# A new order of operations in the nine sparse steps of a cross-attention and mixture-of-experts kernel

## The chip, the cores and the metric

The kernel runs on one core of a Trainium2 chip. A core has five engines with queues of their own: TensorE (matmuls and transposes, written to PSUM), VectorE, ScalarE, GpSimd, and SyncE, which issues DMAs; GpSimd and ScalarE issue some too. They are ordered only by semaphores: an instruction raises a counter when it is done, and another queue waits for a count. The metric is the device time of one execution in microseconds, as the median over several.

## The reference, cut to what matters

```python
x = x + _L0_xattn_ref(_layernorm(x), ctx, ...)   # one head over 1601 context rows
x = x + _L0_ffn_ref(_layernorm(x), ...)          # "B", below
x = x + _L1_xattn_ref(_layernorm(x), ctx, ctx, mask, ...)
x = x + _L1_ffn_ref(_layernorm(x), ...)

def _L0_ffn_ref(x, w_q, w_k, w_gate, value_experts, output_experts):   # HEADS, DIM_HEAD, EXPERTS = 8, 64, 8
    q, k = x @ w_q, x @ w_k                      # 8 heads of 64
    gates = sigmoid(x @ w_gate)                  # an expert for each token and head
    gm = one_hot(argmax(gates)) * gates
    values = einsum('bhne,ehdk,bnd->bhnk', gm, value_experts, x)
    attn = softmax(causal(q * SCALE @ k.T))
    out = einsum('bhij,bhjk->bhik', attn, values)
    return einsum('bhne,ehkd,bhnk->bhnd', gm, output_experts, out).sum(axis=1)
```

x is 4 x 512 x 256. Each token and head picks one of 8 value experts and one of 8 output experts, the same for both.

## The kernel before

The program goes through five stages one after another; the change lies in `attentions_ab` (L439), which does the first attention (A) and B for the four batches in turn. The order of each engine's queue is written out by hand.

**Batches and steps.** Batch b does `attention_a`, then `attention_b`. B takes the 8 heads as four pairs; a step p handles pair p, and Q = 4b + p numbers the steps. In batches 0 to 2, steps 0 to 2 are `sorted_pair` (the nine sparse steps) and step 3 is `last_pair`, which runs beside the start of the next batch's attention A. Batch 3 applies the output experts densely (`pair`, `ending_pair`).

**What a sparse step does on TensorE** (`sorted_pair`, L1214): it turns step p's exponentials (`turn_b`, six parts through PSUM banks 3 and 4), multiplies them with the values (`values`, bank 5), turns the result back (`turn_rows`, bank 4), makes the scores of step p+1 (`scores_b`, three parts, banks 0 and 1), and makes the next step's values for all eight experts in eight units (`unit`, four matmuls of 512 columns). In sparse steps every unit writes bank 2 and waits until VectorE has read the unit before it (`pe.wait_ge(val_mul, U)`, L1112). Between these it turns the sorted rows of step Q-1 (`turn_sorted`, three parts, banks 3 and 4) and multiplies them with the experts' blocks (`out_sorted`, six chunks, banks 6 and 7).

**VectorE** reads units (a product with the gates, L1579, then a sum over experts, L1583), copies parts 1, 3 and 5 of the turned attention (`turned_b`, L1759), reduces the scores' maxima (`maxima`, L1570), makes the rows' weights (`weigh`, L1664, L1668), writes the weighted rows (`write_rows`, L1678, which raises `rows_v`), adds gathered rows to x (`add_back`, L1688, two additions for each of four token tiles), and in step 0 works out where each row goes (`place`, pieces 1 at L1647 to L1653 and 2 at L1658). **ScalarE** copies parts 0, 2 and 4 (L1421), the turned sorted rows (`read_sorted`, L1426) and `boT`, the attention's result (L1474), takes exponentials (`probabilities`, L1413), and copies and stores the chunks (`read_blocks`, L1443, L1446).

**The way of the sorted rows.** When `rows_v` says that step Q's rows are written, GpSimd scatters them to DRAM in the order of their experts (`scatter`, eight indirect DMAs, L716); SyncE loads them as `inS` (`load_sorted`, L628, shown as oxB<-sorted_in); in step Q+1 TensorE turns and multiplies them; ScalarE stores the chunks; in step Q+2 and after GpSimd gathers each token's rows (`gather`, L733), and VectorE adds them. In GpSimd's queue a step is gather (two tiles of Q-2), scatter of Q, gather (the other two). Each gather waits until an earlier one's buffer has been added. In SyncE's queue `load_experts` (L617) issues 22 copies of expert blocks ahead of each `load_sorted`.

The waits that matter, in `values` and in `unit`:

```python
pe.wait_ge(pT_a, 3 * (Q + 1))            # ScalarE's copies, parts 0, 2, 4
pe.wait_ge(pT_v, 3 * (Q + 1))            # VectorE's copies, parts 1, 3, 5
if p == 0 and b < SORTED:
    pe.wait_ge(placed, PLACING * b + 6)  # place piece 1, its first result
...
if u >= 2 * NT:
    pe.wait_ge(val_mul, U)               # VectorE's product of the unit before
```

Of the kernel before, what the change touches and what calls it, by code (L numbers as in the profile page):

```python
# [38 lines left out]
PAIRS = HB // 2  # L39
SORTED = NB - 1  # L40
# [398 lines left out]
def attentions_ab(k, A):  # L439
# [37 lines left out]
    EARLIER = PAIRS * SORTED  # L477
    with ExitStack() as own:
# [321 lines left out]
        def _(pe):  # L800
# [198 lines left out]
            def turn_rows(b, p):  # L999


                Q = PAIRS * b + p
                pe.wait_ge(bo_ev, Q + 1)
                pe.wait_ge(pT_v, 3 * (Q + 1))
                if Q:
                    pe.wait_ge(sorted_a, 3 * (Q - 1) + 2)
                for t in range(NT):
                    mm = pe.transpose(ps[:, 4, t * P:(t + 1) * P], boT[:, t * P:(t + 1) * P], k.ident[:, :])
                mm.then_inc(rows_mm, 1)

            def turn_sorted(Q, g):
# [6 lines left out]
                else:  # L1018
                    pe.wait_ge(exped, NT * (Q // PAIRS + 2))
                    pe.wait_ge(pt_v, 2 * NT * (Q // PAIRS + 2))  # L1020
                if g == 2:
                    pe.wait_ge(sorted_a, 3 * Q + 1)
# [191 lines left out]
            def sorted_pair(b, p):  # L1214
# [9 lines left out]
                if Q:  # L1224
                    turn_sorted(Q - 1, 0)
                scores_b(b, p + 1, 0)
                unit(b, u + 2)
                values(b, p)
                if Q:
                    turn_sorted(Q - 1, 1)  # L1230
                unit(b, u + 3)
                turn_rows(b, p)
                if Q:
# [118 lines left out]
        def _(act):  # L1352
# [96 lines left out]
            def attention_b(b):  # L1449
# [11 lines left out]
                for p in range(PAIRS):  # L1461
# [3 lines left out]
                    if behind:  # L1465
                        read_sorted(Q - 1, 0)
                    if more:
                        probabilities(b, p + 1, 0)
# [3 lines left out]
                    elif Q:  # L1472
                        act.wait_ge(gated, EB * (Q - EARLIER))
                    nc.scalar.copy(boT[:, :], ps[:, 5, :]).then_inc(bo_ev, 1)  # L1474
                    if behind:
                        read_sorted(Q - 1, 1)
# [25 lines left out]
        def _(v):  # L1502
# [328 lines left out]
            def sorted_pair(b, p):  # L1831
# [5 lines left out]
                turned_b(b, p, 5)  # L1837
                weigh(b, p)
                maxima(b, p + 1, 0)
                if p == 0:  # L1840
                    place(b, 1)
                unit(b, u + 2)
                if p and Q >= 3:
                    add_back(Q - 3, 2)
                    add_back(Q - 3, 3)
                if p == 0:
                    place(b, 2)
                unit(b, u + 3)
                write_rows(b, p)
                unit(b, u + 4)  # L1850
# [1368 lines left out]
```

## Time and profile before

| | us |
|---|---|
| median of 3 runs | 2068.59 (2065.03 to 2076.61) |
| profiled execution, its own time | 2065.59 |
| its span in the profile | 2063.6 |
| TensorE busy | 1900.1 (92%) |
| VectorE busy | 1241.6 (60%) |
| ScalarE busy | 980.4 (48%) |
| GpSimd busy | 751.0 (36%) |
| mean granted TensorE clock | 0.973 |
| first sparse step starts, last one ends | 221.8, 771.8 |

A row of the timeline is the start, the length, the engine (PE is TensorE, DVE VectorE, ACT ScalarE, POOL GpSimd, SPq SyncE's queue), the line, the operation with output and input, its shape and count; brackets hold the idle time before it and what ended it. Consecutive instructions of one line are merged. A TensorE row's length includes the way through the array, so the next row can start before it ends; the distance of starts is what an operation takes of the queue. The program's names are those of buffers that several tiles share: oxB holds experts' blocks, rows, `inS`; og_or_pT holds the turned sorted rows and places; val_or_prob the values and the gathered rows; vx_or_keys the value experts. The granted clock is given as a share of full speed.

### The profile page before, as it was taken

Reading aid. Unit: us, or ns where it says so; the run is one execution under the profiler, and the core shown is the slowest. Engines: PE = TensorE matmul, PEld = TensorE weight load, DVE = VectorE, ACT = ScalarE, POOL = GpSimd, SP = SyncE. Lnnn points to the kernel's source line nnn. Section 1 sums busy time; section 2 is a strip of 40 time slices with the busy share of each in tenths; the row PEclk is TensorE's granted clock in tenths of the full one; section 3 lists DMA queues with packets and bytes.
Section 4 is the critical chain, followed back from the end, with each engine's and each line's share of the span. In section 5 each row is a group of like instructions: output and inputs, shape, how many; then the busy total and the mean of one; then the engine's idle time right before and its main releaser. Section 6 shows DMA issues by size and latency. Waiting matters only on the chain. (4 is left out here: it accounts for less than half of the span.)

```text
span 2063.6 us, 29289 instructions
## 1 busy us (share of the span) xinstructions
PE 1900.1 (92%) x10024; PEld 1008.8 (49%) x10024; DVE 1241.6 (60%) x2514; ACT 980.4 (48%) x1899; POOL 751.0 (36%) x702
## 2 busy tenths in 40 slices
PE   8989898999899998899989999999999999986993
PEld 5666445744475446646643333433433343335772
DVE  5423753366535663388777777778777777742332
ACT  3412243224422343221138888778877977951220
POOL 4221335225532453111044233326433621426674
PEclk9999999999999999999999999999999999987997
DMA  8841147217621464422236383345345532114987
GB/s 286 221 169 64 49 153 243 70 29 221 199 99 48 141 207 159 159 48 78 32 98 124 103 245 78 83 96 153 84 82 138 119 58 40 57 58 160 300 177 166
DMA packets 166028, 262.87 MB, mean 127 GB/s; under 512 B 46983, under 2 KB 105173, under 8 KB 164600
## 3 DMA queue, kind: packets, MB, share of 16 engines
q1 hardware_dynamic: 121208, 179.21, 32.1%
q0 software_dynamic: 26624, 47.18, 9.1%
q10 hardware_dynamic: 18048, 34.61, 4.6%
q8 instruction: 80, 1.31, 0.3%
q14 instruction: 68, 0.56, 0.1%
HBM read 165.92 MB, written 104.44 MB: 131 GB/s over the span
## 5 line engine op out<-in xcount | busy, mean ns | idle before, releaser
L2672 ACT ACTIVATE d_prob<-ps 128x512 f32<-128x512 f32 (+1 forms) x832 | 473.6, 597 | 153.1 <-PE ps L2522 152.4
L2699 DVE CUSTOM_DVE_ANT_0 ps<-ps,maskN 128x801 f32<-128x801 f32 x480 | 467.5, 1015 | 122.9 <-PE ps L2492 122.7
L1114 PE MATMUL ps<-vx_or_keys,b_xT 128*128 128x512 f32 x512 | 244.5, 605 | 7.8 <-DVE val_or_prob L1579 7.4
L2534 PE MATMUL ps<-d_prob,vaug 128*32 128x512 f32 (+1 forms) x1664 | 225.9, 609 | 0.3 <-ACT d_prob L2672 0.3
L2521 PE MATMUL ps<-maskT,identb 128*128 128x512 bf16 (+1 forms) x498 | 191.7, 385 | 3.8 <-POOL maskT L2396 1.9
L266 POOL DMA_INDIRECT table<-xr,slot x128 | 128.1, 1000 | 168.4 <-PE ps L2522 130.7
L2668 ACT CAST ps<-maskT 128x512 f32<-128x512 bf16 (+1 forms) x310 | 185.5, 598 | 0.0
L733 POOL DMA_INDIRECT val_or_prob<-sorted_out,oxB x96 | 98.7, 1028 | 186.7 <-DVE xx L1688 114.0
L1579 DVE TENSOR_TENSOR val_or_prob<-ps,b_gm 128x512 f32<-128x512 f32 x128 | 88.3, 690 | 97.5 <-PE ps L1114 97.4
L1413 ACT ACTIVATE prob_or_gate<-ps,b_mx 128x512 f32<-128x512 f32 (+3 forms) x128 | 66.1, 525 | 152.5 <-DVE b_mx L1570 145.4
L716 POOL DMA_INDIRECT sorted_in<-oxB x96 | 95.6, 996 | 116.7 <-issue 57.1
L1114 PEld LDWEIGHTS ps<-vx_or_keys,b_xT 128*128 128x128 f32 x512 | 89.7, 190 | 97.8 <-issue 75.5
L1583 DVE TENSOR_REDUCE val_or_prob<-val_or_prob 128x64 f32<-128x512 f32 x128 | 132.5, 1035 | 4.4
L2396 POOL TENSOR_SCALAR maskT<-c_rawT 128x512 bf16<-128x512 int32 (+1 forms) x52 | 100.1, 1925 | 49.5 <-PE ps L2522 44.2
L2522 PE MATMUL ps<-raw,kS 99*128 99x512 bf16 (+1 forms) x312 | 116.1, 388 | 1.4 <-ACT ps L2668 1.4
L2521 PEld LDWEIGHTS ps<-maskT,identb 128*128 128x128 bf16 (+1 forms) x498 | 49.6, 100 | 120.4 <-issue 33.6
L1443 ACT COPY og_or_pT<-ps 128x1024 f32<-128x1024 f32 x66 | 62.2, 942 | 84.1 <-PE ps L1048 79.6
L2522 PE MATMUL ps<-qS,vx_or_keys 99*128 99x512 bf16 (+1 forms) x260 | 98.6, 383 | 1.9 <-ACT ps L2668 1.9
L2522 PE MATMUL ps<-vx_or_keys 99*128 99x512 bf16 (+1 forms) x260 | 98.3, 382 | 1.9 <-ACT ps L2668 1.9
L816 PE MATMUL ps<-maskN,kS 128*128 128x512 f32 (+1 forms) x256 | 96.5, 523 | 1.7 <-PEq L104 1.7
L848 PE MATMUL ps<-og_or_pT,raw 128*128 128x128 f32 (+1 forms) x832 | 97.6, 275 | 0.0
L848 PEld LDWEIGHTS ps<-og_or_pT,raw 128*128 128x128 f32 (+1 forms) x832 | 95.4, 192 | 1.5 <-issue 1.5
(357 smaller groups left out, 3156.1 us busy)
## 6 DMA issues: line engine op xcount, KB each, us to landing
sorted_out<-og_or_pT ACTq DMA_DIRECT2D x55, 512.0 KB, 3.1
oxB<-in_B_ox SPq DMA_DIRECT2D x264, 64.0 KB
c_rawT<-in_maskT SPq DMA_DIRECT2D x24, 512.0 KB
vx_or_keys<-k_parts SPq DMA_DIRECT2D x60, 200.1 KB, 7.2
k_parts<-x_k SPq DMA_DIRECT2D x16, 600.4 KB
table<-xr POOLq DMA_DIRECT2D x16, 578.0 KB
e_buf<-table SPq DMA_DIRECT2D x32, 289.0 KB, 3.7
oxB<-sorted_in SPq DMA_DIRECT2D x12, 704.0 KB, 6.3
```

What stands on the lines that cost most here:

```text
L266: g.indirect_dma_start(out=k.table[:, :], out_offset=bass.IndirectOffsetOnAxis(ap=k.slot[:, j:j + 1], axis=0), in_=k.xr[:, t, :], in_offse ...
L733: g.indirect_dma_start(out=back[:, t % 2, a, :], out_offset=None, in_=k.sorted_out[Q % 2][:, :], in_offset=bass.IndirectOffsetOnAxis(ap=to ...
L848: mm = pe.matmul(ps[:, 6, m * P:(m + 1) * P], k.ctxNA[0:KW[i], i, m * P:(m + 1) * P], pT[0:KW[i], i, :], start=i == 0 and m == 0, stop=i = ...
L1114: mm = pe.matmul(ps[:, bank, :], xTB[:, c, t * P:(t + 1) * P], vxB[:, c, h, :], start=c == 0, stop=c == NC - 1)
L1583: v.tensor_reduce(val[:, t, h // 2 % 2, h % 2, :], tmp[:, u % 2, :].rearrange("p (e d) -> p d e", e=EB), AX_X, ALU.add).then_inc(val_sum, 1)
L2396: g.tensor_scalar(maskT[0:KW[i], i, :], rawT[0:KW[i], u % 2, i % 2, :], 0.0, MASKED, ALU.is_equal, ALU.mult).then_inc(biasT, 1)
L2521: pe.matmul(ps[0:w, BANKS[u], :], k.identb[0:w, 0:w], maskT[0:w, i, :], start=True, stop=False)
L2522: pe.matmul(ps[0:w, BANKS[u], :], kS[G % NS][0:KROWS + 3, h, i * P:i * P + w], qS[G % NS][0:KROWS + 3, h, :], start=False, stop=True, skip ...
L2534: mm = pe.matmul(ps[VW * h:VW * (h + 1), ACC, :], vaug[0:w, G % 2, i, h, :], prob[0:w, T % 2, h, :], start=i == 0, stop=i == NKT - 1)
L2668: nc.scalar.copy(ps[0:w, BANKS[later], :], maskT[0:w, i, :]).then_inc(mask_a, 1)
L2672: nc.scalar.activation(prob[0:w, T % 2, h, :], ps[0:w, BANKS[GH * T + h], :], ACT.Exp, scale=SCALE_C).then_inc(exped, 1)
L2699: v.tensor_tensor_reduce(banks, banks, maskN[:, t, MO[half]:MO[half] + w], 1.0, -3.0e38, ALU.add, ALU.max, mp[:, t, h, half:half + 1]).the ...
```

## The change

It changes the order inside `sorted_pair` on TensorE and VectorE, and of two operations in ScalarE's loop.

- TensorE: `values` goes ahead of the scores' first part, `turn_rows` follows the scores, and then come unit u+2, `turn_sorted` 1, unit u+3, `turn_sorted` 2 and unit u+4. `turn_rows` writes the bank that `turn_sorted` 1 uses, so it now waits only for the sorted rows of the step before last (except in `last_pair`), and `turn_sorted` 1 waits for `write_rows`.
- ScalarE: in batches 0 to 2 the copy to `boT` goes ahead of the exponentials of the scores' first part.
- VectorE: `place` 1 goes ahead of `weigh`; the left additions of step Q-3 (tiles 2 and 3) go ahead of the maxima; `write_rows` goes behind the maxima and ahead of unit u+2.

```diff
@@ -1003,7 +1003,7 @@
                 pe.wait_ge(bo_ev, Q + 1)
                 pe.wait_ge(pT_v, 3 * (Q + 1))
                 if Q:
-                    pe.wait_ge(sorted_a, 3 * (Q - 1) + 2)
+                    pe.wait_ge(sorted_a, 3 * (Q - 1) + (2 if p == PAIRS - 1 else 0))
                 for t in range(NT):
                     mm = pe.transpose(ps[:, 4, t * P:(t + 1) * P], boT[:, t * P:(t + 1) * P], k.ident[:, :])
                 mm.then_inc(rows_mm, 1)
@@ -1018,6 +1018,8 @@
                 else:
                     pe.wait_ge(exped, NT * (Q // PAIRS + 2))
                     pe.wait_ge(pt_v, 2 * NT * (Q // PAIRS + 2))
+                if g == 1 and (Q + 1) % PAIRS < PAIRS - 1 and Q + 1 < EARLIER:
+                    pe.wait_ge(rows_v, Q + 2)
                 if g == 2:
                     pe.wait_ge(sorted_a, 3 * Q + 1)
                 for i, j in enumerate(range(4 * g, min(4 * g + 4, BLOCKS))):
@@ -1223,13 +1225,13 @@
                 turn_b(b, p, 5)
                 if Q:
                     turn_sorted(Q - 1, 0)
+                values(b, p)
                 scores_b(b, p + 1, 0)
+                turn_rows(b, p)
                 unit(b, u + 2)
-                values(b, p)
                 if Q:
                     turn_sorted(Q - 1, 1)
                 unit(b, u + 3)
-                turn_rows(b, p)
                 if Q:
                     turn_sorted(Q - 1, 2)
                 unit(b, u + 4)
@@ -1464,7 +1466,7 @@
                     read_turned(Q)
                     if behind:
                         read_sorted(Q - 1, 0)
-                    if more:
+                    if more and b == SORTED:
                         probabilities(b, p + 1, 0)
                     act.wait_ge(bpv_mm, Q + 1)
                     if 1 <= Q <= EARLIER:
@@ -1472,6 +1474,8 @@
                     elif Q:
                         act.wait_ge(gated, EB * (Q - EARLIER))
                     nc.scalar.copy(boT[:, :], ps[:, 5, :]).then_inc(bo_ev, 1)
+                    if more and b < SORTED:
+                        probabilities(b, p + 1, 0)
                     if behind:
                         read_sorted(Q - 1, 1)
                         read_sorted(Q - 1, 2)
@@ -1835,18 +1839,18 @@
                 turned_b(b, p, 3)
                 unit(b, u + 1)
                 turned_b(b, p, 5)
-                weigh(b, p)
-                maxima(b, p + 1, 0)
                 if p == 0:
                     place(b, 1)
-                unit(b, u + 2)
+                weigh(b, p)
                 if p and Q >= 3:
                     add_back(Q - 3, 2)
                     add_back(Q - 3, 3)
+                maxima(b, p + 1, 0)
+                write_rows(b, p)
+                unit(b, u + 2)
                 if p == 0:
                     place(b, 2)
                 unit(b, u + 3)
-                write_rows(b, p)
                 unit(b, u + 4)
                 maxima(b, p + 1, 1)
                 unit(b, u + 5)
```

## Rows read from the trace of the kernel before

**Rows 1.** The page's first part: busy time of each engine.

```profile
PE 1900.1 (92%) x10024; PEld 1008.8 (49%) x10024; DVE 1241.6 (60%) x2514; ACT 980.4 (48%) x1899; POOL 751.0 (36%) x702
```

**Rows 2.** TensorE's waits, 225 to 900 us: total, times, longest.

```profile
PE ps L1024 <- DMA oxB<-sorted_in: 9.4, 5, 2.5
```

**Rows 3.** TensorE's timeline in batch 1, step 1: start, length, instructions, idle before.

```profile
475.83 1.98 PE L1114 MATMUL ps<-vx_or_keys,b_xT 128*128 128x512 f32 x4 [0.15 <-DVE val_or_prob L1579]
...
483.48 0.63 PE L1024 MATMUL ps<-ident,oxB 128*128 128x128 f32 x4 [0.33 <-ACT b_pT L1421]
484.04 1.13 PE L957 MATMUL ps<-b_kT,b_qT 64*128 64x512 f32 x4
...
485.22 1.94 PE L1114 MATMUL ps<-vx_or_keys,b_xT 128*128 128x512 f32 x4
487.09 2.37 PE L1083 MATMUL ps<-b_pT,val_or_prob 128*64 128x512 f32 x16
489.39 0.66 PE L1024 MATMUL ps<-ident,oxB 128*128 128x128 f32 x4
489.89 1.88 PE L1114 MATMUL ps<-vx_or_keys,b_xT 128*128 128x512 f32 x4
491.61 0.60 PE L1008 MATMUL ps<-ident,b_oT 128*128 128x128 f32 x4
492.04 0.49 PE L1024 MATMUL ps<-ident,oxB 128*128 128x128 f32 x3
492.55 1.98 PE L1114 MATMUL ps<-vx_or_keys,b_xT 128*128 128x512 f32 x4
```

**Rows 4.** VectorE's timeline in the same step.

```profile
484.20 0.55 DVE L1759 COPY b_pT<-ps 128x384 f32<-128x384 f32 x1
...
485.42 1.23 DVE L1570 TENSOR_REDUCE b_mx<-ps 128x2 f32<-128x1024 f32 x1 [0.36 <-PE ps L962]
487.20 0.69 DVE L1579 TENSOR_TENSOR val_or_prob<-ps,b_gm 128x512 f32<-128x512 f32 x1 [0.55 <-PE ps L1114]
...
488.89 1.86 DVE L1688 TENSOR_TENSOR xx<-xx,val_or_prob 128x256 f32<-128x256 f32 x4
...
493.49 0.68 DVE L1678 TENSOR_TENSOR oxB<-ps,b_gr 128x512 f32<-128x512 f32 x1
```

**Rows 5.** ScalarE's timeline in the same step.

```profile
489.51 0.59 ACT L1474 COPY b_oT<-ps 128x512 f32<-128x512 f32 x1 [1.32 <-PE ps L1083]
```

**Rows 6.** TensorE's timeline at two of the five waits for sorted rows.

```profile
258.99 0.66 PE L1024 MATMUL ps<-ident,oxB 128*128 128x128 f32 x4 [2.48 <-DMA oxB<-sorted_in]
...
548.41 1.11 PE L1024 MATMUL ps<-ident,oxB 128*128 128x128 f32 x4 [1.63 <-DMA oxB<-sorted_in]
549.32 2.90 PE L816 MATMUL ps<-maskN,kS 128*128 128x512 f32 x4
```

**Rows 7.** TensorE's, then VectorE's timeline in batch 0, step 0.

```profile
228.31 0.82 PE L983 MATMUL ps<-ident,prob_or_gate 128*128 128x128 f32 x6
...
237.71 1.99 PE L1114 MATMUL ps<-vx_or_keys,b_xT 128*128 128x512 f32 x4 [0.35 <-DVE val_or_prob L1579]
...
230.17 0.55 DVE L1759 COPY b_pT<-ps 128x384 f32<-128x384 f32 x1
...
232.08 0.41 DVE L1647 SCALAR_TENSOR_TENSOR og_or_pT<-og_or_pT,ps 128x256 f32<-128x256 f32 x1
```

**Rows 8.** SyncE's queue, expert copies and the sorted load behind them.

```profile
255.12 28.57 SPq L617 DMA_DIRECT2D oxB<-in_B_ox  x22
286.45 0.37 SPq L628 DMA_DIRECT2D oxB<-sorted_in  x1
```

**Rows 9.** GpSimd's timeline, last gather behind batch 1, step 0's scatter.

```profile
479.60 1.01 POOL L733 DMA_INDIRECT val_or_prob<-sorted_out,oxB  x1 [0.30 <-issue]
```

**Rows 10.** Windows: PE, PEld, DVE, ACT, POOL busy (instructions), granted clock, DMA share, GB/s.

```profile
548.00:552.00 4.00, 3.59 (x8) 1.92 (x8) 0.82 (x2) 0.59 (x1) 0.00 (x0) 0.58 0.68 243
258.00:262.00 4.00, 3.01 (x13) 1.47 (x14) 1.41 (x4) 0.59 (x1) 0.00 (x0) 1.00 0.22 62
```

## The prediction

> **What bounds the kernel now.** The first part of the page says that TensorE is busy for 1900.1 of 2063.6 us [rows 1], so an edit counts only where it moves TensorE. The change touches only the nine sparse steps (batches 0 to 2, steps 0 to 2, 221.8 to 771.8 us) and, through its transfers, the last step of each batch. So I read the list of what TensorE waited for from 225 to 900 us, then its timeline through one step, then VectorE's and ScalarE's timelines beside it, then the queues of GpSimd and SyncE that bring the sorted rows back.
>
> The list shows five waits of 9.4 us in total for the sorted rows, before `turn_sorted` part 0 [rows 2]. They stand at 259.0 (2.48 us), 324.0 (2.49), 548.4 (1.63), 712.9 (0.38) and 777.8 (2.42); two are shown [rows 6]. They are all that earlier rows can give back. The other waits of a step (two transposed banks, the sorted chunks' copies) are not touched.
>
> Step 1 of batch 1 shows the pattern. TensorE goes from `turn_sorted` 0 (483.48) through scores, unit u+2, values, `turn_sorted` 1, unit u+3, the rows and `turn_sorted` 2 to unit u+4 at 492.55 without a wait [rows 3]: 9.07 us. The old order uses the scores and a unit to cover VectorE's last copy of transposed attention (484.20 to 484.75) [rows 4], and uses values and the rows to keep units u+2, u+3 and u+4 apart. All three share PSUM bank 2, so each waits for VectorE's product of the one before.
>
> **The change, part by part.** I walk the same step in the new order with the same rows.
>
> *Values ahead of the scores.* `turn_sorted` 0 lets the next operation start at 484.04. Values needs VectorE's copy of part 5, which ends at 484.20 + 0.55 = 484.75; TensorE follows such a release after 0.05 us (VectorE's product at 0.04 us after a unit's end is the same size). Values starts at 484.80: **0.76 us new**.
>
> *Rows ahead of the unit.* Values takes 2.30 us to the next start (487.09 to 489.39), scores 1.18 (484.04 to 485.22), the rows 0.43 (491.61 to 492.04) [rows 3]. Scores start at 487.10, the rows at 488.28, unit u+2 at 488.71. ScalarE's copy of the attention (0.59 us) [rows 5] starts when values ends, at about 487.2, and is over by 487.8, before the rows need it: it now stands ahead of the exponentials, so nothing is ahead of it. The exponentials move behind it and are wanted only by the scores' second part, some 8 us later. No cost.
>
> *Units closer together.* Unit u+2 ends 1.88 us after its start [rows 3, 4], at 490.59. The product runs 490.63 to 491.32 (0.69 us) and frees bank 2 at 491.37. TensorE, with only `turn_sorted` 1 between (unit 1.72 to the next start, transposes 0.50), is there at 490.93: **0.44 us new**. A unit after a wait lasts 1.98 us (475.83), so u+3 ends at 493.35, its product at 494.08, and u+4 starts at 494.13, while u+3 (1.72 to the next start) and `turn_sorted` 2 (0.51) would let it start at 493.60: **0.4 to 0.5 us new**. Before it started at 492.55. The step is 1.6 us longer, and from u+4 on nothing differs: units and chunks there are released by the same copies in the same order.
>
> *VectorE's moves.* The maxima start 1.38 us after the scores (484.04 to 485.42) and take 1.23 [rows 4], so they run 488.48 to 489.71 and `write_rows` (0.68) ends at 490.4. The new wait of `turn_sorted` 1 on these rows (TensorE at 490.43) is about met, the narrowest term: if write_rows is late by x, x comes on top, but u+3 hides the first 0.44. Behind it stand only those transposes and the units. The left additions (four, 1.86 us from 488.89) [rows 4] now follow the weights at about 485.1 and end by 487.0, inside the time until the maxima can start. Their last gather was issued by 480.6 [rows 9] and stands behind the step before's scatter, which also moves up, and no wait was seen on them. I take them at nothing; had the rows landed only at 488.9, the maxima would end some 2 us late in four steps, 6 us in all. Done earlier, they let GpSimd's next gather, and the scatter queued behind it, start some 4 us earlier.
>
> *Step 0 of a batch.* Values also waits for `place` 1's first result, which now comes right behind the copy. That operation takes 0.41 us [rows 7], 0.33 more than the copy alone, since neighbours on VectorE overlap by about 0.09: 1.9 us for step 0 of batches 1 and 2. In the very first step there is no `turn_sorted`. The transposes leave TensorE free at 228.31 + 0.74 = 229.05, the copy ends at 230.72, the result at 231.04: 2.04 us of idling. With no transposes between the units either, u+2 starts at 235.0, u+3 at 237.65 and u+4 at 240.4 in place of 237.71 [rows 7]: 2.7 us.
>
> Sum of the new waits: 2.7 + 2 x 1.9 + 6 x 1.6 = **16.1 us**.
>
> *What comes back.* `write_rows` moves from 493.49 to about 489.7 within its step, so scatter and load may move 3.8 us. But SyncE issues 22 expert copies (28.57 us, 255.12 to 283.69) ahead of the load, which went out at 286.45 once the scatter had landed [rows 8]; it can move at most 2.8 us there. TensorE itself arrives later: at 258.99 - 2.48 + 2.7 = 259.2 for the first wait [rows 6], past even the old landing; 3.4, 5.1, 1.9 and 4.7 us later at the others. So all five waits go: **-9.4 us**. One of them was followed by a stretch at a granted clock of 0.58, between the two levels of 1.2 and 2.4 GHz [rows 10]: the next batch's scores at 549.32 last 2.90 where four such matmuls last 1.88. With the transposes (1.11 for 0.66) that costs 1.4 us [rows 6]. The stretch around 259, after the 2.48 us wait, stays at 1.00. I count its loss as a gain, **-1.4 us**, between 0 and 1.4.
>
> Between batches, TensorE waits 2.37 us at 582.9 for GpSimd's normalised tile. That waits for the last stored chunk, which moves with TensorE, so it stays.
>
> Net: 16.1 - 9.4 - 1.4 = **+5.3 us**. The profiled execution took 2065.59 us (span 2063.6); the sum makes it 2070.9. The median of the runs is 3.0 us above the profiled one, so the predicted median is 2068.6 + 5.3 = **2073.9 us**, 0.26% more. The three runs lie 11.6 us apart; about 0.5% (10.3 us) is what a measurement of this kernel can tell from no change.
>
> **Rivals.** (a) *The short waits cost TensorE its clock, and it is slower.* The place is the stretch from `turn_sorted` 0 to u+4, where each step's waits grow by 1.6 us. One such stretch at 0.58 costs 1.4 us by [rows 6, 10]; with one in each of the nine steps it is 13 us more, 2087. It passes 0.5% from four such steps on. For it: the 1.63 us wait did so. Against it: the 2.48 us wait did not. Chance 0.13.
> The Trainium skill, "TensorE: Matmul & The Clock Gate", section "A second HAM failure mode: psum-queue depth-cycling", says that short idling between groups of matmuls that cycle through banks makes the clock swing and lowers throughput. By that rule this change, which makes a single bank the pace of three units, would be rival (a). By the rows of the steps, which wait at bank 2 already, it would be my sum.
>
> (b) *The bank does not pace the units.* Only the wait before values is real: 6 x 0.76 + 2 x 1.09 + 2.04 = 8.8 us, minus 10.8: 2066.6, no change. For it: the copies and products on which it rests are a few tenths apart, and missing records could hide slack. Against it: the same release is seen at 475.83 with 0.15 us, where one short chunk stands between units. Chance 0.17.
>
> (c) *The transfers come no earlier and TensorE still waits at them.* The load stands behind 22 expert copies; if these start later as the step grows, the five waits stay: 2068.6 + 16.1 = 2084.7. It decides when a load lands over 3 us later after its step's start than now. Against it: a step is longer by less than TensorE's arrival moves. Chance 0.06.
>
> (d) *No new wait at all*, the transposed attention being ready in time: 2068.6 - 10.8 = 2057.8. The copy's end at 484.75 speaks plainly against it. Chance 0.03.
>
> **Numbers.** The forecast has 0.61, with its own range of 2067 to 2081 (bounds: a clock stretch more or less at 1.4 us each, narrow waits a few tenths in nine steps, up to 6 us for the additions). To leave out no more than 2 in 10, the range runs over (b) and most of (a) and (c): 2062 to 2085. Faster by over 0.5% (under 2058.3): (d) and a tail of (b), 0.05. Slower (over 2078.9): most of (a), all of (c) and the tail of the forecast, 0.18. Same 0.77.
>
> **What would show it.** In the changed profile, values should wait 0.6 to 0.8 us for VectorE's transposed copy in eight steps and about 2 in the first; units u+3 and u+4 should each show 0.2 to 0.45 us behind VectorE's product; the wait for sorted rows before part 0 should be gone; steps should run some 34.5 us where 32.9 stands now; the load should go out right behind the 22nd expert copy. The prediction is wrong if turn_sorted 1 waits for `write_rows` by much more than 0.2 us (then maxima or additions are late), if load waits persist, or if the granted clock in the steps falls under 0.95.

## The result, and the profile after

The changed kernel took 2095.11 us (median of 4 runs, 2084.77 to 2104.28) and the kernel before, beside it, 2066.81 (2064.11 to 2076.61). The ratio is 1.0133, with a 95% interval of 1.0100 to 1.0166: 1.3% slower, outside the range of the prediction. The profiled execution took 2097.95 us. The four runs of the changed kernel spread with the clock: the fastest had a mean granted clock of 0.973, the slowest 0.965.

The page's first part for the changed kernel (busy time of each engine) answers to [rows 1]:

```profile
PE 1903.9 (91%) x9944; PEld 1017.9 (49%) x10024; DVE 1242.0 (59%) x2514; ACT 979.6 (47%) x1899; POOL 752.8 (36%) x702
```

TensorE does the same work in a span of 2096.0 us in place of 2063.6. The time lies in what it waited for, from 225 to 900 us, in the same view as [rows 2] (total, times, longest):

```profile
PE ps L983 <- ACT og_or_pT L1445: 16.5, 6, 5.0
PE ps L1116 <- DVE val_or_prob L1583: 13.0, 25, 1.2
...
PE ps L1085 <- issue: 4.5, 6, 0.8
PE ps L1085 <- DVE og_or_pT L1651: 4.3, 3, 2.1
```

The same view of the kernel before has these two lines for the first and the second:

```profile
PE ps L1114 <- DVE val_or_prob L1579: 5.5, 9, 1.2
...
PE ps L983 <- ACT og_or_pT L1443: 2.3, 3, 0.8
```

The wait for the sorted rows, 9.4 us before, has left the list. The waits of units and of values have grown as forecast. The first line was not in the forecast: the first transposes of a step (`turn_b` 0) wait 16.5 us for ScalarE's copy of the sixth chunk, where they waited 2.3. ScalarE in turn waits for the landing of its own stores, 20.4 us in 8 places; the second line is the kernel before:

```profile
ACT og_or_pT L1445 <- DMA sorted_out<-og_or_pT: 20.4, 8, 4.3
```

```profile
ACT og_or_pT L1443 <- DMA sorted_out<-og_or_pT: 1.5, 1, 1.5
```

**Inside a step it went as worked out.** TensorE's timeline in batch 1, step 1 of the changed kernel, which answers to [rows 3]:

```profile
493.78 0.63 PE L1026 MATMUL ps<-ident,oxB 128*128 128x128 f32 x4 [0.33 <-ACT b_pT L1423]
495.16 2.37 PE L1085 MATMUL ps<-b_pT,val_or_prob 128*64 128x512 f32 x16 [0.75 <-issue]
497.46 1.13 PE L957 MATMUL ps<-b_kT,b_qT 64*128 64x512 f32 x4
498.52 0.29 PE L962 MATMUL ps<-causal,identb 128*128 128x128 bf16 x2
498.64 0.61 PE L1008 MATMUL ps<-ident,b_oT 128*128 128x128 f32 x4
499.09 1.88 PE L1116 MATMUL ps<-vx_or_keys,b_xT 128*128 128x512 f32 x4
500.81 0.63 PE L1026 MATMUL ps<-ident,oxB 128*128 128x128 f32 x4
501.75 1.98 PE L1116 MATMUL ps<-vx_or_keys,b_xT 128*128 128x512 f32 x4 [0.31 <-DVE val_or_prob L1583]
503.57 0.49 PE L1026 MATMUL ps<-ident,oxB 128*128 128x128 f32 x3
504.52 1.98 PE L1116 MATMUL ps<-vx_or_keys,b_xT 128*128 128x512 f32 x4 [0.46 <-DVE val_or_prob L1583]
```

Values waits 0.75 us. The list calls this wait "issue", but VectorE's copy of part 5 ends 0.1 us before its end (494.51 + 0.55 = 495.06), as forecast:

```profile
494.51 0.55 DVE L1763 COPY b_pT<-ps 128x384 f32<-128x384 f32 x1
```

Unit u+3 waits 0.31, unit u+4 0.46, and `turn_sorted` 1 at 500.81 waits for nothing. The step's units start at 486.12 and the next step's at 520.73: 34.6 us, where the prediction had some 34.5.

**At the end of a step it did not.** First TensorE, then ScalarE at the end of batch 0, step 2 and the start of step 3 of the changed kernel:

```profile
325.66 0.70 PE L1050 MATMUL ps<-oxB,og_or_pT 64*128 64x256 f32 x4
329.68 1.06 PE L983 MATMUL ps<-ident,prob_or_gate 128*128 128x128 f32 x7 [3.32 <-ACT og_or_pT L1445]
330.99 3.44 PE L983 MATMUL ps<-ident,prob_or_gate 128*128 128x128 f32 x13 [0.25 <-ACT b_pT L1423]
334.22 1.06 PE L1026 MATMUL ps<-ident,oxB 128*128 128x128 f32 x4
335.07 2.96 PE L816 MATMUL ps<-maskN,kS 128*128 128x512 f32 x4
```

```profile
322.66 0.37 ACTq L1448 DMA_DIRECT2D sorted_out<-og_or_pT  x1
323.93 1.01 ACT L1445 COPY og_or_pT<-ps 128x1024 f32<-128x1024 f32 x1 [1.30 <-DMA sorted_out<-og_or_pT]
...
328.95 0.59 ACT L1445 COPY og_or_pT<-ps 128x512 f32<-128x512 f32 x1 [2.55 <-DMA sorted_out<-og_or_pT]
```

The sixth chunk has been multiplied at 326.36 (325.66 + 0.70). ScalarE copies it only at 328.95, because it copies into two buffers by turns, and this chunk's still holds the fourth chunk until its store, issued at 322.66, has landed: 6.2 us later (328.9). `turn_b` 0 waits for all copies of the step before (`pe.wait_ge(blocks_a, CHUNKS * (Q - 1))`), so TensorE waits too. The reason is in SyncE's queue, which answers to [rows 8]:

```profile
292.91 28.16 SPq L617 DMA_DIRECT2D oxB<-in_B_ox  x22
321.19 0.54 SPq L628 DMA_DIRECT2D oxB<-sorted_in  x1
```

The load of the sorted rows (704 KB) goes out right behind the 22nd expert copy, as forecast, and so ahead of the stores of the fourth, fifth and sixth chunk. The view of DMA issues (KB each, median us from issue to landing) shows it, for 12 us at this place of the changed kernel (318 to 330), then of the kernel before (309 to 321):

```profile
sorted_out<-og_or_pT ACTq DMA_DIRECT2D x3, 512.0 KB, 5.6
oxB<-sorted_in SPq DMA_DIRECT2D x1, 704.0 KB, 6.1
```

```profile
sorted_out<-og_or_pT ACTq DMA_DIRECT2D x3, 512.0 KB, 2.9
oxB<-sorted_in SPq DMA_DIRECT2D x1, 704.0 KB, 6.7
```

The three 512 KB stores of the changed kernel are those of the third, fourth and fifth chunk. The third's was issued at 319.98, 1.2 us ahead of the load, and landed after 3.9 us; the two behind the load took 6.2 and 5.6. In the kernel before, the load went out at 317.24, 0.6 us before the next step's first transposes, and behind all three of these stores, the last of which was issued at 315.63.

**The granted clock** (level 2.4 GHz at 1.00; 1.2 GHz would be 0.50) fell behind some of these waits. Windows of the changed kernel, with the columns of [rows 10]:

```profile
234.70:239.00 4.30, 4.25 (x18) 2.13 (x20) 1.07 (x4) 0.14 (x1) 0.00 (x0) 0.60 0.17 49
329.50:338.00 8.50, 7.93 (x30) 5.23 (x30) 3.69 (x9) 2.17 (x5) 1.02 (x1) 0.60 0.30 93
493.00:506.00 13.00, 11.15 (x54) 5.50 (x51) 9.20 (x15) 4.05 (x9) 7.09 (x7) 1.00 0.34 102
```

The first lies behind the 2.06 us wait of the first step, the second behind the 3.32 us wait, and the third, with waits of 0.33, 0.75, 0.31 and 0.46, keeps its clock. I laid windows of 8 us over the whole stretch from the first sparse step's first transposes to batch 3's and added length times (1 - clock): 11.8 us before, 22.1 after. Of the latter 10.2 us stand behind the three long waits at `turn_b` (3.32 us at 329.68, 5.04 at 560.94 and 4.57 at 800.04); at these transposes the kernel before loses none. The other differences, each of 1.7 us or 3.4, cancel: new are the first step and two places near 600 and 822, gone are the load wait's at 548 and one near 407.

The 32.4 us by which the span grew are 24.9 in this stretch (677.8 to 702.7), 3.6 ahead of it and 3.9 behind it, where both kernels run the same instructions. The 3.6 are clock: from 185 to 200 us it is 0.77 in this profile and 1.00 in that of the kernel before. So a part of a profile's clock loss comes and goes between executions, whatever the order of the steps.

The length of a wait does not settle by itself whether the clock falls behind it. All versions with values ahead of the scores have the same 2.06 us wait in the first step. First the changed kernel, then run 1 below:

```profile
234.75 4.07 PE L1085 MATMUL ps<-b_pT,val_or_prob 128*64 128x512 f32 x16 [2.06 <-DVE og_or_pT L1651]
```

```profile
231.42 2.37 PE L1087 MATMUL ps<-b_pT,val_or_prob 128*64 128x512 f32 x16 [2.06 <-DVE og_or_pT L1653]
```

Values takes 2.37 or 2.38 us in the profiles of runs 1, 2, 3 and 6, and 4.07 and 4.06 in the changed kernel's and run 5's, which are also the two of these six with 0.77 at 185 to 200 us. Why that is so stays open.

### The profile page after: what moved, and what is told of

Same layout as the page of the kernel before. It is cut to its first block and busy times, and to the rows that moved or that the text cites. A ratio compares the mean times of both kernels' runs of the same rounds, so it can differ in the third digit from the quotient of the medians.

```text
span 2096.0 us, 29217 instructions
## 1 busy us (share of the span) xinstructions
PE 1903.9 (91%) x9944; PEld 1017.9 (49%) x10024; DVE 1242.0 (59%) x2514; ACT 979.6 (47%) x1899; POOL 752.8 (36%) x702
## 5 line engine op out<-in xcount | busy, mean ns | idle before, releaser
L1116 PE MATMUL ps<-vx_or_keys,b_xT 128*128 128x512 f32 x512 | 244.8, 606 | 15.0 <-DVE val_or_prob L1583 14.4
L2525 PE MATMUL ps<-maskT,identb 128*128 128x512 bf16 (+1 forms) x425 | 163.6, 385 | 1.8 <-DVE d_oN L2735 1.7
```

Of the source, the lines that this page charges most:

```text
L1116: mm = pe.matmul(ps[:, bank, :], xTB[:, c, t * P:(t + 1) * P], vxB[:, c, h, :], start=c == 0, stop=c == NC - 1)
L2525: pe.matmul(ps[0:w, BANKS[u], :], k.identb[0:w, 0:w], maskT[0:w, i, :], start=True, stop=False)
```

## The experiments

Three theories went in. **Theory 1**: the early load shares the transfers' bandwidth with the last chunk stores, and a full store buffer passes the delay on to TensorE. **Theory 2**: the left additions, moved ahead, move the gathers, and these hold ScalarE's copies up. **Theory 3**, rival (a) of the prediction: the short waits in the steps cost the clock. Diffs are against the changed kernel where nothing else is said.

**1. The load held behind the last chunk** (SyncE, ahead of the load):

```diff
+                    if p < PAIRS - 1:
+                        sp.wait_ge(blocks_mm, CHUNKS * Q)
                 sp.dma_start(inS, ...)
```

> The changed kernel, with one more wait in SyncE's queue: in steps 0 to 2 the load of the sorted rows goes out only when TensorE has finished the last chunk of the step before. Theory 1 (the load, 704 KB and now issued some 3 us ahead of the last two chunk stores, makes these stores land late; ScalarE's copy of the last chunk waits for a buffer, and the next step's first transposes wait for that copy): the 16.5 us of waits before the first transposes fall to about 2.3 us as in the kernel before, the waits for the sorted rows come back in the three last steps (about 2.3 us each), and the time falls by 10 to 15 us, to about 2080 us. Theory 2 (GpSimd's gathers and scatters, which moved up too, slow the stores): the waits stay near 16 us and the time near 2095 us. Theory 3 (the clock alone costs it): neither the waits nor the time change.

Measured: 2085.49 us against 2070.2, ratio 1.0056 (1.0034 to 1.0078). TensorE's waits in its profile:

```profile
PE ps L1028 <- DMA oxB<-sorted_in: 8.4, 6, 2.8
...
PE ps L985 <- ACT og_or_pT L1447: 2.4, 3, 0.9
```

The 16.5 us are back at 2.4, and the load waits at 8.4. ScalarE's waits for its stores are back at 2.9 us in 3 places. The gathers and additions keep their places (at the end of batch 0, step 2 the first gather is issued 0.57 us behind the fourth chunk's first matmul in both kernels, at 316.21 and 321.00), and the 512 KB stores there take 3.6 us in place of 5.6. So it is the early load that makes `turn_b` wait, and not the gathers.

**2. The additions back behind unit u+2.**

```diff
-                if p and Q >= 3: add_back(Q - 3, 2); add_back(Q - 3, 3)   # ahead of the maxima
+                if p and Q >= 3: add_back(Q - 3, 2); add_back(Q - 3, 3)   # behind unit(b, u + 2)
```

> The changed kernel with the left additions of step Q-3 back behind unit u+2. Gathers and scatters of steps 5, 6, 9 and 10 start some 5 us later and so does the load behind them; step 2 of batch 0 has no such additions. Theory 1 (load against stores): the 3.3 us wait at the end of batch 0 stays, those of batches 1 and 2 (1.4, 5.0, 1.75, 4.6 us) shrink to near zero, in all 8 to 12 us less, about 2085 us. Theory 2 (gathers against stores): the gathers of tiles 2 and 3 of the step before last move back too, so all shrink but batch 0's, which cannot be told from theory 1 here; the two differ in the first experiment. Theory 3: no change from 2095 us.

Measured: 2086.9 us, ratio 1.0079 (1.0048 to 1.0110). The wait at `turn_b` is 5.8 us in 4 places, a load wait of 6.1 us is there again, and ScalarE's copies wait 11.4 us in 4 places for gathers, which they hardly do in the changed kernel:

```profile
PE ps L1026 <- DMA oxB<-sorted_in: 6.1, 2, 3.2
PE ps L983 <- ACT og_or_pT L1445: 5.8, 4, 2.6
...
ACT og_or_pT L1445 <- DMA val_or_prob<-sorted_out,oxB: 11.4, 4, 3.7
```

With the additions late, GpSimd reaches the scatter late, the load goes out later and collides less: in the last steps of batches 1 and 2 the wait at `turn_b` is 0.78 us and the load waits are 3.15 and 2.97; in batch 0, which has no such additions, `turn_b` still waits 2.57 us, where I had expected 3.3. Both theories forecast that the waits shrink, so this run alone does not tell them apart. With run 1 it says that the moved additions let the load go early enough to cause the wait.

**3. The rows back behind unit u+3, values still ahead.**

```diff
                 scores_b(b, p + 1, 0)
-                turn_rows(b, p)
                 unit(b, u + 2)
                 if Q: turn_sorted(Q - 1, 1)
                 unit(b, u + 3)
+                turn_rows(b, p)          # write_rows on VectorE likewise
```

> The changed kernel with the turned rows and write_rows back behind unit u+3 (values still ahead of the scores, the copy of the attention and the additions still early). The rows are written about as late as before, so scatter and load are late again. Theory 1: no chunk waits beyond 2.3 us; in each step 0.74 us before values, 0.3 us before unit u+3, none before u+4; with waits for the sorted rows of some 2 us in the last steps: about 2067 + 9 to 12 = 2076 to 2079 us. Theory 2: the gathers ahead of the scatter are still early, so part of the chunk waits stay: 2085 us or more.

Measured: 2082.19 us, ratio 1.0051 (1.0036 to 1.0066). The wait at `turn_b` is 2.3 us in 3 places, the load waits 9.7 in 5, values' waits 7.3, units' 8.3. Without the earlier rows, nothing of the new wait is left, and neither is anything of the gain. The time is some 3 us above what I had expected.

**4. The kernel before, with the additions alone moved ahead of the maxima** (the second diff the other way round, in the kernel before).

> The kernel before with only the left additions ahead of the maxima. GpSimd's gathers of steps 5, 6, 9 and 10 start some 4 us earlier, the scatter only 1 us (write_rows ends at 494.2 there). Theory 1: the load goes out 1 us earlier at most, the chunk waits stay near 2.3 us and the time within 4 us of 2067 us. Theory 2: early gathers alone bring chunk waits of several us, 2072 us or more.

Measured: 2070.85 us, ratio 0.9999 (0.9982 to 1.0016); load waits 10.2 us in 4 places, `turn_b` 2.3 in 3. Alone, this edit costs nothing and brings nothing.

**5. A buffer of its own for the sixth chunk** (512 floats a partition that nothing uses in these steps; not shown is a wait on VectorE that keeps the next batch's attention A from overwriting it before its store has landed):

```diff
+                own_buffer = c == 5 and (Q + 1) % PAIRS < PAIRS - 1 and not between
-                if n >= 2:
+                if n >= 2 and not own_buffer:
                     act.wait_ge(kept[c % 2], 16 * (n // 2))
-                o = outS[not between][c % 2]
+                o = last_out if own_buffer else outS[not between][c % 2]
```

> The changed kernel, with the sixth chunk of each sparse step copied to a buffer of its own, so that ScalarE's copy of it no longer waits for the store of the fourth chunk. The load goes out as early as in the changed kernel and meets the stores as before. Theory 1 (the early load delays the stores, and a store buffer that is not free delays the sixth copy and with it the next step's first transposes): TensorE's wait at turn_b for ScalarE's chunk copy falls from 16.5 us in 6 places to under 6 us, while the landing of the stores stays near 5.6 us where the load runs; the stretches of low clock behind the waits go as well, and the time falls by 8 to 14 us against the changed kernel, to 2081 to 2087. Rival (ScalarE reaches the sixth chunk late for another reason, as the exponentials behind the attention's copy or the gathers): the waits at turn_b stay above 12 us and the time stays at 2093 to 2097.

Measured: 2075.18 us (10 runs) against 2069.0, ratio 1.0029 (1.0007 to 1.0051). The chunk copy's line in TensorE's list, and the place of the 3.32 us wait:

```profile
PE ps L984 <- ACT og_or_pT L1447: 2.3, 3, 0.8
...
327.28 0.96 PE L984 MATMUL ps<-ident,prob_or_gate 128*128 128x128 f32 x7 [0.78 <-ACT og_or_pT L1447]
328.58 2.32 PE L984 MATMUL ps<-ident,prob_or_gate 128*128 128x128 f32 x13 [0.35 <-ACT b_pT L1424]
```

The load still goes out early (321.56) and the stores still take long (median 6.8 us from issue to landing between 318 and 334), but TensorE no longer waits for them, and ScalarE's waits for them fall from 20.4 us to 2.7. The 13 transposes take 2.32 us in place of 3.44, and of the clock loss in the stretch (22.1 us) 13.6 are left, none of them behind the first transposes. This is the decisive run: 16.5 us went to 2.3 by a buffer, and the ratio from 1.0133 to 1.0029, further than the 2081 to 2087 us that I had expected. The prediction's own sum, +0.26%, lies within its interval, which reaches from 0.07% to 0.51%. Its profile is of the slowest of the ten executions (2082.41 us).

**6. The x_mid store held until the last chunk is multiplied.** In step 2 of batches 1 and 2, SyncE issues a 512 KB store behind the load.

```diff
                         if p == 2 and b >= 1:
+                            sp.wait_ge(blocks_mm, CHUNKS * (PAIRS * b + p))
                             keep_x(b - 1)
```

> The changed kernel, with the 512 KB store of x_mid (step 2 of batches 1 and 2) held until TensorE has done the step's last chunk; the load of the sorted rows stays early. Theory 1 says that both transfers are in the way: the waits of 5.0 and 4.6 us at the start of the last steps of batches 1 and 2 fall to about 3.3, that of batch 0, which has no x_mid store; in all 16.5 goes to about 13.5, and the time to 2090 to 2094. Rival, the load alone is the cause: the waits stay at 5.0 and 4.6 and the time at 2095. Rival, the x_mid store is most of it: they fall under 1.5 us.

Measured: 2084.81 us, ratio 1.0096 (1.0071 to 1.0120); `turn_b` waits 11.9 us in 6 places, longest 3.3:

```profile
PE ps L984 <- ACT og_or_pT L1446: 11.9, 6, 3.3
```

The two longest waits (5.0 and 4.6) are gone to the level of batch 0, where there is no such store. So about 5 of the 16.5 us are the second transfer's. Against the kernel before, the time is 19.9 us longer in place of 27.5, so it fell by 7.6 us where I had expected 1 to 5, though the two intervals overlap. Behind those two waits the clock had fallen too (loss in the stretch 22.1 us after, 15.3 here).

**7 and 8. Another order, with and without the third buffer**, against the kernel before. Scores stay ahead of values; the rows go to bank 5, which values has left:

```diff
                 scores_b(b, p + 1, 0)
-                unit(b, u + 2)
                 values(b, p)
+                unit(b, u + 2)
+                turn_rows(b, p)          # bank 5; the next values waits for rows_v Q
                 if Q: turn_sorted(Q - 1, 1)
                 unit(b, u + 3)
-                turn_rows(b, p)
```

On VectorE `write_rows` follows unit u+2; the additions, `place` 1 and ScalarE's copy of the attention stay as early as in the changed kernel.

> A version of the kernel before that aims at the load waits alone. Scores stay ahead of values; unit u+2 follows values and the rows follow it, written to bank 5, which values has left, so that turn_sorted 1 need not wait for them; write_rows stands behind unit u+2 on VectorE, the left additions and place 1 ahead of the maxima, the copy of the attention ahead of the exponentials, and the sixth chunk has a buffer of its own. By the in-step walk: no wait before values, 0.43 us before u+4 in nine steps (3.9 us), write_rows about 2.3 us earlier than before, so the load leaves 2 us earlier and the five load waits (9.4 us) fall to under 2; with the stretch of low clock gone, 5 to 7 us faster than before, 2060 to 2065. If an early load costs even with the third buffer, or units are paced another way, it is the same as before or slower, 2066 to 2075.

> The same without the buffer of its own for the sixth chunk. Theory 1: the load is only 2 us earlier than in the kernel before and meets just the last one or two stores, so the waits at turn_b for the chunk copy are 2 to 6 us, more than in the kernel before (2.3) and less than in the changed one (16.5); the time is 0 to 4 us above the version with the buffer. Rival, the number of buffers does not matter: both versions take the same time and show the same waits at turn_b.

Measured: with the buffer 2072.0 us, ratio 1.0011 (0.9989 to 1.0032); without it 2069.99, ratio 1.0013 (0.9996 to 1.0029). The 4 us in front of u+4 are there in both (units' waits 9.2 and 9.8 us). A gain in time is not. With the buffer the load waits are 8.1 us in 4 places, without it 3.2 in 5. The wait at `turn_b` is 2.3 and 2.4 us, so here the number of buffers makes no difference, as the rival said, and the 2.4 us without it lie at the low end of what I had expected. SyncE's queue and TensorE at the last of them, with the buffer:

```profile
775.85 0.36 SPq L629 DMA_DIRECT2D oxB<-sorted_in  x1
776.27 2.22 SPq L604 DMA_DIRECT2D x_mid<-kS  x1
```

```profile
786.55 0.66 PE L1025 MATMUL ps<-ident,oxB 128*128 128x128 f32 x4 [3.58 <-DMA oxB<-sorted_in]
```

Issue to use is 10.7 us, where the kernel before had 6.4 at this place (771.40 to 777.79). Against the start of the step it was issued 3.1 us earlier (3.5 us ahead of it in place of 0.4) and used 1.2 us later (7.2 us behind it in place of 6.0). I had expected it to bring the waits under 2 us, and that was wrong: in this profile, beside stores and the x_mid store, the earlier issue was no earlier landing. It need not be so. Without the buffer the load went out as early at this place (770.23, 3.3 us ahead of the step), landed after 5.8 us, and nothing waited; there the stores took 8.8 us. That the two versions differ in this rests on one profile each, and I don't lay it to the buffer.

**9 to 12. On another chip.** The last runs fell on a chip where the kernel before itself takes 2190.14 us (2207.57 beside the last one), so they are read against runs of that chip alone.

Run 9 adds the suspected cause to the kernel before and moves nothing:

```diff
+                if Q and p < PAIRS - 1:
+                    sp.wait_ge(blocks_mm, CHUNKS * (Q - 1) + 4)
+                    sp.dma_start(k.x_mid[NB - 1], <512 KB of constants>).then_inc(extra, 16)
                 for half in scattered[Q % 2]: ...      # then the load
```

> The kernel before with one suspected cause added and nothing moved: in eight sparse steps SyncE issues a store of 512 KB (constant data to a DRAM buffer that is overwritten later) right behind the expert copies, when the fourth chunk has been multiplied, so some 3 us ahead of the load of the sorted rows. Theory 1 (a large transfer beside the last chunk stores delays them, and the full store buffer holds up the sixth copy and the next step's first transposes): the stores land about 1.3 us later (512 KB at some 390 GB/s), TensorE's wait at turn_b for the chunk copy rises from 2.3 us in 3 places to 5 to 12 us in 5 to 8 places, and the time by 3 to 12 us. Rival, that wait needs the changed order of copies and exponentials on ScalarE: it stays at 2.3 us and the time within 2 us, but for load waits that may grow by up to 1 us each.

Runs 10 to 12 hold the x_mid store until the load has landed, in the kernel before (10) and in the version of run 8 (11, and 12 once more):

```diff
                         if p == 2 and b >= 1:
+                            sp.wait_ge(ld_sorted, 16 * (PAIRS * b + p + 1))
                             keep_x(b - 1)
```

> The kernel before, with the x_mid store of batches 1 and 2 held until the load of the sorted rows has landed (they are issued 0.4 us apart). If transfers issued together share the bandwidth, the load lands about 1 us earlier in these two steps: the load waits at 548.4 (1.63 us) and 777.8 (2.42) fall to 0.5 to 1.4, and the low-clock stretch behind the first may go; 1 to 4 us faster, not to be told from no change. Rival: the load's landing does not depend on the store, and nothing moves.

> The version with the rows in bank 5 and two buffers, with the x_mid store held until the load has landed. Load waits fall from 3.2 us in 5 places to 1.5 to 2.5, and the waits at turn_b stay at 2.4; 2065 to 2070, the same as the kernel before within what can be told.

> The version with the rows in bank 5, two buffers and the x_mid store behind the load once more, in five rounds, on whatever chip is free. If it gains only where transfers are slow (the chip of the run before took 2190 us for the kernel before), then on a chip where the kernel before takes 2065 to 2070 us it is the same within 0.3%: load waits 9.4 to some 2 us, 4 us new before u+4, and 0 to 3 us more or less at the batch's end. If the gain of 1.0% is the version's own, it is 2045 to 2055.

Measured: run 9 2205.19 us, ratio 1.0051 (1.0018 to 1.0083); run 10 2182.03, 0.9961 (0.9921 to 1.0002); run 11 2162.05, 0.9896 (0.9811 to 0.9981); run 12 2169.8 against 2207.57, 0.9814 (0.9770 to 0.9858). The `turn_b` wait in run 9, and in run 10 (from 225 to 960 us), which is nearest to the kernel before on this chip:

```profile
PE ps L990 <- ACT og_or_pT L1450: 16.5, 8, 4.8
```

```profile
PE ps L1049 <- ACT og_or_pT L1444: 42.8, 19, 9.6
PE ps L1049 <- issue: 33.5, 11, 7.8
...
PE ps L984 <- ACT og_or_pT L1444: 6.0, 5, 1.6
```

An extra transfer ahead of the last stores raises the wait from 6.0 us in 5 places to 16.5 in 8, with no order changed, and the kernel is slower by 11 us (0.51% of 2190). ScalarE's copies wait 23.5 us for their own stores in place of 16.5, and 8.8 for gathers in place of 1.9. That has the sign and the size of Theory 1, but it weighs less than runs 1, 5 and 6: run 10 is only a stand-in for a profile of the kernel before on this chip, and this chip has waits of its own. `out_sorted` waits 76.3 us in run 10 (42.8 + 33.5), and ScalarE's list for the whole span of run 10 names something as the end of its idle time that the kernel before never shows on the first chip in its list:

```profile
ACT og_or_pT L1444 <- remote: 114.2, 19, 11.7
```

Such waits end late though the input is there ("remote" is the list's name for a releaser that the trace does not hold). In run 10 TensorE has done its scores at 584.78 (584.38 + 0.40), and VectorE starts their maxima at 593.46:

```profile
584.38 0.40 PE L963 MATMUL ps<-causal,identb 128*128 128x128 bf16 x4
```

```profile
593.46 1.29 DVE L1571 TENSOR_REDUCE b_mx<-ps 128x2 f32<-128x768 f32 x2 [9.15 <-remote]
```

What holds the engines up there I could not find in the profile; it stays open.

Run 10 moved nothing that can be told (its interval ends at 1.0002). Runs 11 and 12 gain 1.0% and 1.9%. Their version was not run on a chip where the kernel before takes 2069 us; its sister without the moved store (run 8) took the same time there as the kernel before, and moving the store alone (run 10) is worth 0.8% at most here. So the gain most likely belongs to this chip, but that is not shown. It comes with this chip's waits: those of `out_sorted` are 53.0 us in run 12 (32.6 + 20.4) for 76.3 in run 10. Why this version has fewer of them was not tried apart.

## Why the prediction was wrong

The step that failed is the reading that TensorE's end of a step stays as it is. It stands twice: "The other waits of a step (two transposed banks, the sorted chunks' copies) are not touched", and in *Units closer together*: "The step is 1.6 us longer, and from u+4 on nothing differs: units and chunks there are released by the same copies in the same order." The chunk copies are also released by their stores' landing, and *What comes back* moved a 704 KB load to before these stores while it counted only what TensorE gains from that. Of a moved transfer I had asked when it lands, and not what it delays. The runs put +14.2 us of waiting in its place (16.5 for 2.3), and in the profile 10.2 us of lost clock behind the three longest of them. Taken away with a buffer (run 5), the waits go and the loss in the stretch is 13.6, and +5.3 us forecast stands beside +6.0 measured (0.29% of 2069, with an interval of 1.4 to 10.6 us). That the two lie so near is in part luck, since the clock gain of 1.4 us in the sum was not there.

Term by term, from the lists of waits between 225 and 900 us, against the kernel before, in us. "In the step" is the growth of the waits of units and values, "chunk" that of `turn_b` for the chunk copy, "load" that of `turn_sorted` 0; "measured" is the ratio less 1, times the time of the kernel before it was measured beside.

| | in the step | chunk | load | sum | measured |
|---|---|---|---|---|---|
| the change | 15.8 | 14.2 | -9.4 | 20.6 | 27.5 |
| 5, third buffer | 15.9 | 0.0 | -9.0 | 6.9 | 6.0 |
| 6, x_mid late | 14.4 | 9.6 | -9.4 | 14.6 | 19.9 |
| 1, load behind the chunks | 14.4 | 0.1 | -1.0 | 13.5 | 11.6 |
| 2, additions back | 17.5 | 3.5 | -3.3 | 17.7 | 16.4 |
| 3, rows late | 9.6 | 0.0 | 0.3 | 9.9 | 10.6 |
| 4, additions only | 0.0 | 0.0 | 0.8 | 0.8 | -0.2 |
| 7, rows in bank 5, third buffer | 4.0 | 0.0 | -1.3 | 2.7 | 2.3 |
| 8, rows in bank 5 | 4.6 | 0.1 | -6.2 | -1.5 | 2.7 |

The sum of the three gives the time within 4.2 us, but for the change and run 6, which lie 6.9 and 5.3 above it. These are the two with chunk waits of 3.3 us and more, behind which the clock fell. The "chunk" column is what is new at the first transposes. In the changed kernel 3.8 us of it only replaced waits for the copies inside `turn_b` (6.9 us for VectorE's and 4.2 for ScalarE's before, 3.9 and 3.4 after, and again 6.9 and 4.2 in run 5). So the whole list grew by 17.8 us (52.1 to 69.9), and not by 20.6.

- **New waits in the step, 16.1 us**: right, 15.8. The first step too: values waits 2.06 us at 234.75 (2.04 forecast).
- **The first step's clock**: not in the sum. Values took 4.07 us there in place of 2.37, at a granted clock of 0.60: 1.7 us, in this profile and in run 5's, but not in those of runs 1, 2, 3 and 6 behind the same wait.
- **Load waits, -9.4 us**: right, all five are gone.
- **Clock, -1.4 us**: wrong in sign. The loss behind the load wait at 548.4 went, but there are new ones behind the longer waits at `turn_b`.
- **Additions and `write_rows` at no cost**: right. The additions run from 495.28 to 497.15, the maxima start at 498.85, `write_rows` ends at 500.67, and `turn_sorted` 1 at 500.81 does not wait.
- **Between batches, no change**: right, 2.0 us for 2.4.
- **Rival (a)**, clock lost to short waits, had the wrong place. The steps with their 1.6 us of new waits kept 1.00; what lost it was the 2.06 us wait of the first step, in this profile, and the waits of 3.32 us and more at the starts of the last steps. Rivals (b), (c) and (d) fall by the rows above.

That two transfers issued by two engines are in each other's way is also what the Trainium skill says in "DMA: Bandwidth & Descriptors", section "Issuing engines are not separate DMA queues": whichever engine starts them, they run on the same 16 DMA engines and interleave. The trace agrees: the load is in SyncE's queue, the stores in ScalarE's, and the stores landed a median of 5.6 us after their issue in place of 2.9.

By "TensorE: Matmul & The Clock Gate" of the Trainium skill (section "A second HAM failure mode: psum-queue depth-cycling"), short idling between groups of matmuls that cycle through banks makes the clock swing. No run here shows that for these steps; their window, 493 to 506 us, is at 1.00 with one bank pacing three units.

## What to carry to other kernels

When an edit lets a large transfer start earlier, ask what is in flight at the new moment, and whether any engine waits for that: here 9.4 us of waits for a load were exchanged for 14.2 us of waits for stores that were hidden before, and in the profile for more in clock. Where the profile shows no wait on a transfer, it still shows how much room it has (the store of the fourth chunk had 3.75 us, from 313.38 to its buffer's next use at 317.13, and took 2.9); subtract before moving anything beside it. And a walk through one step that stops where "the order is the same" must go on to the buffers' releases at the end of the step.

## What the runs showed of the hardware

- A load issued earlier can land no earlier: at one place it took 6.3 us from issue to landing before, and 10.7 in run 7 with the issue 3.1 us earlier against its step, beside the last chunk stores and a 512 KB store. Run 8, issued as early beside the same transfers, took 5.8, and its stores 8.8.
- Stores of 512 KB went from a median of 2.9 us to 5.6 when a 704 KB load was issued among them: 6.2 and 5.6 us for the two behind it.
- The length of a wait alone does not say whether the clock falls. The same 2.06 us wait of the first step was followed by values at half pace (4.07 and 4.06 us) in two profiles and at full pace (2.37 or 2.38) in four; of waits for the sorted rows, one of 1.63 us lost clock in the kernel before and three of 2.42 to 2.49 did not. Four waits of 0.31 to 0.75 us in 13 us left it at 1.00.
- Chips differ by more than any edit here: the medians of the kernel before were 2067 to 2070 us in three sets of runs and 2190 and 2208 in two others, with idle times of up to 12 us that no engine or transfer of the core explains. An order that was worth nothing in the first, with one store moved as well, took off 1.0% and 1.9% there.
